# One decoder layer on one core: the last bulk rows requested behind the last regrouping, and three engines' orders rearranged

## What is computed

```
x = layernorm(x + scan_block(x))            # W_in, conv, scan over 16 states, W_out
hn = mlstm(q=x, k=ctx, v=ctx)               # decay matrix, normalizer, norm of each head, times outnorm
x = layernorm(x + hn)
logits = x @ gate_w                         # (2048, 8)
mult, sel = sparse_mixer(logits)            # top 2 experts of a token and their gates
h   = silu(x @ w1[e]) * (x @ w3[e])         # 256 -> 1024, for each expert e
out = layernorm(x + sum over 2 picks of mult * (h @ w2[e]))
```

## Time and profile before

| | us |
|---|---|
| median of the runs | 667.14 (665.72 to 668.47) |
| the profiled execution | 670.12 |
| its span, first to last instruction | 668.6 |
| PE busy | 587.2 (88%) |
| DVE busy | 456.7 (68%) |
| POOL busy | 287.2 (43%) |
| ACT busy | 249.0 (37%) |
| mean granted clock of PE | 0.926 |

### The profile page before, as it was taken

The page is one execution under the profiler, slowest core; times in us unless marked ns, Lnnn a source line. Parts: engine busy times, 40 slices in busy tenths (PEclk is TensorE's granted clock), DMA queues, the critical chain, the costliest instruction groups (busy, mean ns, idle before and its releaser), DMA issues.

```text
span 668.6 us, 13885 instructions
## 1 busy us (share of the span) xinstructions
PE 587.2 (88%) x3498; PEld 458.0 (69%) x3499; DVE 456.7 (68%) x1368; ACT 249.0 (37%) x477; POOL 287.2 (43%) x211
## 2 busy tenths in 40 slices
PE   6999989699699888537898989999999999999980
PEld 2444568588356666435687878888888888888870
DVE  2566487956566777876774766777677767677672
ACT  3555540001666653222421424224242242422262
POOL 7100020002092446646570674818576167572323
PEclk9999999899879969557899999999999999999985
DMA  8999607201300006222258475865858547544562
GB/s 269 327 335 336 196 1 203 51 1 43 147 2 1 33 9 259 81 81 95 65 132 224 98 212 146 224 157 136 223 123 232 103 94 218 146 91 94 113 195 91
DMA packets 75418, 93.42 MB, mean 140 GB/s; under 512 B 15869, under 2 KB 70270, under 8 KB 72560
## 3 DMA queue, kind: packets, MB, share of 16 engines
q1 hardware_dynamic: 63280, 78.28, 40.1%
q0 software_dynamic: 6672, 9.58, 7.3%
q10 hardware_dynamic: 5424, 5.05, 3.1%
HBM read 42.93 MB, written 31.67 MB: 112 GB/s over the span
## 4 chain that ended last, share of the span: by engine, by line
PE 63%; DVE 17%; POOL 6%; ACT 4%; DMA 3%; issue 3%; SPq 1%; another core or an unknown queue 1%; POOLq 0%; ACTq 0%; DVEq 0%
PE bank L2408 24%; PE bank L2420 13%; PE bank L1978 8%; PE bank L2137 4%; DMA xcol<-xcol 2%; POOL experts_w L861 2%; DVE region L1383 2%; DVE region L1381 2%; DVE small L1400 1%; PE bank L2028 1%; PE bank L1987 1%; PE bank L2286 1%; POOL small L780 1%; PE bank L1994 1%; PE bank L2242 1%
## 5 line engine op out<-in xcount | busy, mean ns | idle before, releaser
L2408 PE MATMUL bank<-experts_w,experts_x 128*128 (+1 forms) x864 | 215.2, 399 | 2.9 <-issue 2.9
L2408 PEld LDWEIGHTS bank<-experts_w,experts_x 128*128 128x128 f32 x864 | 157.3, 188 | 36.5 <-issue 3.7
L2420 PEld LDWEIGHTS bank<-experts_w 128*128 128x128 f32 x840 | 106.5, 194 | 6.6 <-issue 3.7
L2420 PE MATMUL bank<-experts_w 128*128 x840 | 107.7, 285 | 3.1 <-DVE region L1867 1.8
L909 POOL DMA_INDIRECT total<-region,rid x32 | 49.5, 1547 | 113.9 <-DVE region L1867 92.0
L1173 ACT ACTIVATE region<-bank 128x512 f32<-128x512 f32 x72 | 42.3, 597 | 129.2 <-PE bank L2408 115.8
L780 POOL TENSOR_TENSOR small<-small 128x4 f32<-128x4 f32 (+5 forms) x21 | 26.4, 1259 | 112.7 <-DVE small L1392 92.1
L1843 DVE TENSOR_TENSOR xcol<-region,bank 128x512 f32<-128x512 f32 x72 | 49.1, 682 | 37.1 <-ACT region L1173 37.0
L1179 ACT CAST experts_w<-bank 128x512 fp32r<-128x512 f32 x70 | 40.5, 587 | 71.7 <-DVE bank L1852 64.6
L1978 PE MATMUL bank<-xcol,region 128*128 128x512 f32 x128 | 58.1, 612 | 7.4 <-DMA xcol<-in_xT 5.8
L889 POOL TENSOR_TENSOR experts_w<-wstage,experts_w 128x2048 f32 x12 | 55.3, 4625 | 12.8 <-ACT experts_w L1197 12.8
(11 more groups left out here) (368 smaller groups left out, 933.8 us busy)
## 6 DMA issues: line engine op xcount, KB each, us to landing
wstage<-in_w_exp SPq DMA_DIRECT2D x18, 1024.0 KB, 5.2
xcol<-xcol SPq DMA_DIRECT2D x140, 128.0 KB
slots<-padrow SPq DMA_DIRECT2D x8, 2210.0 KB, 19.7
wstage<-in_w_exp SPq DMA_DIRECT2D x2, 3072.0 KB, 12.1
region<-slots ACTq DMA_DIRECT2D x34, 130.0 KB
xcol<-in_xT SPq DMA_DIRECT2D x4, 512.0 KB, 6.6
xtok<-in_x SPq DMA_DIRECT2D x1, 2048.0 KB, 13.3
region<-in_ctxT SPq DMA_DIRECT2D x1, 2048.0 KB, 7.6
```

The costliest lines, as they stand in the source:

```text
L2408: mm = pe.matmul(bank[2 * u + m][:, :], (xTh, xTl)[a][:, s, k, :], moving(off, w, m * KD * F + k * F + u * HALF, HALF), start=(k == 0 and ...
L2420: mm = pe.matmul(bank[into][:, 0:D], (high, low)[a][:, u, c, :], moving(off, w, 2 * KD * F + (4 * u + c) * D, D), start=(u == 0 and c == 0 ...
```

## The change

Six things, in the order of the program.

1. POOL's addition in `head_weights(u)` waits for `rexp_in` to reach u, for u = 1 and 2.
2. ACT's `router_exp` stands behind `weigh_keys` in the attention loop.
3. DVE's `route_place(b-2)` stands ahead of `norm2_stats(b-1)`.
4. `ENDS` is now ((0, 2), (2, 4), (6, 4), (10, 4), (14, 2)). SP has a `last_pair` of its own: it leaves out the last `load_ahead`, and requests the four groups right behind the last regrouping.
5. POOL computes the powers of the first two groups ahead of the four gathers of late rows.
6. In the last pair DVE turns block g ahead of the product of the last block, and splits block g around the first norms; ACT's norm rows are dealt out in smaller portions; PE's `last_turn(1)` stands between the two halves of `down(g)`; `end_shift(5)` stands ahead of the last late rows.

No arithmetic is added or removed. Three of the places follow as rows, each before and after. The line numbers of the changed kernel are 3 to 8 higher.

On DVE in the third turn of a sequence (c = 2), before: statistics (`BN_STATS`), then placing.

```diff
--- before.py
+++ after.py
@@ -58,7 +58,7 @@
 LOGITS_AT = {i + 1: b for i, b in TURN_AT.items()}
 RANK_AT = {i + 2: b for i, b in TURN_AT.items()}
 KEEP = 4
-ENDS = ((0, 4), (4, 4), (8, 4), (12, 2), (14, 2))
+ENDS = ((0, 2), (2, 4), (6, 4), (10, 4), (14, 2))
 LATE = 4
 LO_PARTS = 12
 LONG = 2
@@ -627,19 +627,22 @@
                 load_ahead(2 * p - 1)
                 regroup(2 * p, 0)
                 load_ahead(2 * p)
-            all_pairs(sp, pair, pair)
-
-            sp.wait_ge(w_ready, events)
-            sp.sem_inc(sp_gate, 1)
-            even = sp.value_load(tab_n[0:1, 1:2], min_val=2 * SURE - 2, max_val=NB - 2)
-            sp.wait_ge(y_sent[1], 8 * even)
-            sp.sem_inc(sp_gate, 1)
             def rows_of(t, u):
                 first, n = ENDS[u]
                 return t[first * P:(first + n) * P, :].rearrange("(i p) d -> p i d", p=P)
-            for u in range(1, len(ENDS)):
-                first, n = ENDS[u]
-                sp.dma_start(ya[:, first:first + n, :], rows_of(total, u)).then_inc(y_back[u], 16)
+
+            def last_pair(p):
+                regroup(2 * p - 1, 1)
+                load_ahead(2 * p - 1)
+                sp.wait_ge(w_ready, events)
+                sp.sem_inc(sp_gate, 1)
+                regroup(2 * p, 0)
+                sp.wait_ge(y_sent[1], 16 * p)
+                sp.sem_inc(sp_gate, 1)
+                for u in range(1, len(ENDS)):
+                    first, n = ENDS[u]
+                    sp.dma_start(ya[:, first:first + n, :], rows_of(total, u)).then_inc(y_back[u], 16)
+            all_pairs(sp, pair, last_pair)
             for u, (first, n) in enumerate(ENDS):
                 sp.wait_ge(fin_done, u + 1)
                 sp.dma_start(rows_of(out, u), ya[:, first:first + n, :]).then_inc(out_done, 16)
@@ -805,6 +808,8 @@
                 rows = hbuf[:, first % NQ:first % NQ + n].rearrange("p q h d -> p q (h d)")
                 here = xtok[:, first:first + n, 0:D]
                 link(pool.tensor_tensor(rows, rows, bc(onw[:, :], 1, [P, n, D]), ALU.mult))
+                if u:
+                    pool.wait_ge(rexp_in, u)
                 pool.tensor_tensor(here, here, rows, ALU.add).then_inc(resid_done, 1)
 
             def scatter(tiles, g):
@@ -930,11 +935,13 @@
                 pool.wait_ge(y_sent[1], 16 * p)
                 pool.sem_inc(pool_gate, 1)
                 pool.wait_ge(rid_end_done, 1)
+                for u in range(2):
+                    rsqrt(*ENDS[u][::-1])
                 for n in range(LATE):
                     pool.indirect_dma_start(out=ya[:, NT + n, :], out_offset=None, in_=total,
                                             in_offset=bass.IndirectOffsetOnAxis(ap=rid_end[:, n:n + 1], axis=0)).then_inc(gathered[n], 16)
             all_pairs(pool, pair, last_pair)
-            for first, n in ENDS:
+            for first, n in ENDS[2:]:
                 rsqrt(n, first)
             for k in range(0, LATE, 2):
                 rsqrt(2, NT + k)
@@ -1131,12 +1138,12 @@
                     decays(i + 1)
                     if c == NQ - 1:
                         states(b + 1)
-                if i in RANK_AT:
-                    router_exp(RANK_AT[i])
                 if i in TURN_AT:
                     norm2_turned(TURN_AT[i])
                 if b + 1 < B and c in (1, 2):
                     weigh_keys(b + 1, range(3 * c - 3, 3 * c))
+                if i in RANK_AT:
+                    router_exp(RANK_AT[i])
                 if b and c == NQ - 1:
                     norm2_apply(b - 1)
             norm2_turned(B - 2)
@@ -1240,16 +1247,17 @@
                 silu(last, 0)
                 act.wait_ge(grouped[0], 32 * g + 64)
                 act.sem_inc(act_gate, 1)
+                norm_rows(0, 0, 2, True)
                 plain(last, 0)
                 for u in range(2):
                     high_turned(g, u)
-                norm_rows(0, 0, 4, True)
                 silu(last, 1)
+                norm_rows(1, 2, 2, False)
                 high_end(0)
                 plain(last, 1)
-                norm_rows(1, 4, 3, False)
+                norm_rows(1, 4, 1, False)
                 high_end(1)
-                norm_rows(1, 7, 1, True)
+                norm_rows(1, 5, 1, True)
             all_pairs(act, pair, last_pair)
             for u in range(2, len(ENDS)):
                 norm_rows(u, *ENDS[u], True)
@@ -1681,9 +1689,9 @@
                     route_second(b - 2)
                     route_gates(b - 2)
                 if b and c == 2:
-                    norm2_stats(b - 1)
                     if b >= 2:
                         route_place(b - 2)
+                    norm2_stats(b - 1)
                 if b < B - 1 and c == NQ - 1:
                     if b:
                         norm2_scale(b - 1)
@@ -1931,16 +1939,16 @@
                 for u in range(2):
                     low_turned(g - 1, u, bank[4 + u], hTh, hTl)
                 end_stats(0)
-                middle(last, 1, 0)
                 for u in range(2):
                     turn(g, 0, u)
-                for u in range(2):
-                    low_turned(g, u, bank[4 + u], hTh, hTl)
                 end_shift(0)
+                middle(last, 1, 0)
                 end_stats(1)
+                low_turned(g, 0, bank[4], hTh, hTl)
+                end_shift(1)
+                low_turned(g, 1, bank[5], hTh, hTl)
                 middle(last, 1, 1)
                 low_turned(last, 0, bank[0], endTh, endTl)
-                end_shift(1)
                 end_stats(2)
                 low_turned(last, 1, bank[2], endTh, endTl)
                 end_shift(2)
@@ -1952,8 +1960,8 @@
                 end_shift(4)
                 waiting[5] = norm_stats(NT, 2, 1e-5, NT, ya)
                 late_rows(g, 2, 1)
+                end_shift(5)
                 late_rows(last, 3, 3)
-                end_shift(5)
                 waiting[6] = norm_stats(NT + 2, 2, 1e-5, NT + 2, ya)
                 end_shift(6)
             all_pairs(dve, pair, last_pair)
@@ -2481,9 +2489,9 @@
                 up(last, 1, 1, off)
                 last_turn(0)
                 off = offset_of(event_of(g))
-                for u in range(2):
-                    down(g, u, off, hTh, hTl, 1)
+                down(g, 0, off, hTh, hTl, 1)
                 last_turn(1)
+                down(g, 1, off, hTh, hTl, 1)
                 off = offset_of(event_of(last))
                 for u in range(2):
                     down(last, u, off, endTh, endTl, 3)
```

## The result

The changed kernel took 664.85 us (median of 22 runs, 662.59 to 668.21), the kernel before beside it 667.70 us (22 runs, 664.75 to 669.43). The medians are 2.9 us apart; the ratio, taken over all runs, is 0.997, 95% interval 0.9958 to 0.9982: 0.3% faster, 2.0 us, and between 1.2 and 2.8. The prediction had 662.2 us, which is 4.9 us less: the sign was right, the size about twice too large (2.5 times by the ratio, 1.7 by the medians).

What follows compares the result with a forecast made beforehand. PE bounds the expert stage; a relay between engines, with DVE held by POOL, the routing stage. 670.12 less 4.0 (routing) less 0.9 (last stage) is 665.2; the median, 3.0 lower, 662.2 us, range 660.4 to 667.2.

Steps and rivals of the forecast that it cites:

- the last stage: End of the program: earlier turn, mostly spent by a longer DVE tail, leaves 0.9 us gained.
- turn: Last stage: DVE's turn comes at 635.3 instead of 639.54, as less transfer traffic stands beside the regrouping.
- turn to last shift: Last stage: DVE's span behind the turn is 21.0 us, from 635.3 to 656.3; it was 17.90.
- last shift to first final send: Last stage: POOL's final sends also wait for bulk groups landing in out; 1.1 us gain counted as 0.9.
- The tail's work: Last stage: DVE's work behind the turn grows from 15.25 to 16.7 us by a product and larger statistics.
- the wait behind four gathers: Last stage: DVE waits 1.0 us for the power of group 2, behind four gathers on POOL.
- the routing stage: 205 to 277 us: second norm2_scale 4.6 us earlier; 4.0 us reach the stage's end, bounds 2.5 and 5.2.
- Rival (a): Routing stage: the clock falls anyway after 244, giving 2.5 us and not 4.0; 663.7 us, chance 0.18.
- rival (b): Routing stage: POOL's held additions push sends and powers, costing up to 2.1 us; 664.3 us, chance 0.12.
- Between 277 and 622 us: Relay and expert loop, forecast from 277 to 629: only start 4.0 us earlier, nothing moved; 0 us.
- (c): Relay from 277 to 350 ends on something fixed, so only the last stage gains; 666.2 us, chance 0.10.
- (d): Last stage: bulk rows share engines with the regrouping; turn at 642.5, what follows 6.6 late; 668.8 us, chance 0.10.

Runs made afterwards that it cites:

- e9: Kernel before with the three routing edits and, of the last stage, only SP's bulk-row requests right behind the last regrouping; 666.93 us, ratio 0.9949.
- e2: Changed kernel with the three routing edits undone, so the kernel before with the last-stage items only; 670.84 us, ratio 1.0011 to the kernel before.
- e5: The changed kernel, unchanged, run again in the second batch against the kernel before; 668.28 us, ratio 0.9954.
- e8: Whole change with four keep-busy matmuls also ahead of the values groups beside the logits; 671.10 us, ratio 1.0012 to the kernel before.
- e15: The whole change again, unchanged, in the fourth batch against the kernel before; 667.4 us, ratio 0.9967.
- e18: Whole change with placing ahead of norm 2's statistics only in the first sequence (b = 2); 666.49 us, ratio 0.9945 to the kernel before.
- e12: Kernel before with the three routing edits alone, second run of that program; 668.32 us, ratio 0.9985.
- e14: The kernel before, no edit, second copy of the fourth batch, against itself; 670.17 us, ratio 0.9991.
- e13: The kernel before, no edit, first copy of the fourth batch, against itself; 669.96 us, ratio 0.9998.
- e7: Whole change with POOL's four gathers ahead of all powers again; 667.25 us, ratio 0.9956 to the kernel before.
- e6: Whole change with POOL's power of the third group between the second and third gather; 667.35 us, ratio 0.9967 to the kernel before.
- e16: Kernel before with the three routing edits alone, third run of that program; 667.93 us, ratio 0.9977.
- e1: Kernel before with the three routing edits only (items 1 to 3), first run; 666.98 us, ratio 0.9939.
- e4: Kernel before with only POOL's addition waiting for rexp_in; 669.19 us, ratio 0.9961.
- e3: Kernel before with placing and keys moved, POOL's addition not waiting for rexp_in; 670.55 us, ratio 1.0007.
- e10: Kernel before with POOL's wait for rexp_in and the placing moved, keys still behind router_exp; 666.87 us, ratio 0.9958.
- e11: Kernel before with the three routing edits, but POOL's addition waiting for rexp_in only for u = 1; 668.33 us, ratio 0.9969.
- e17: Kernel before with the three routing edits, placing ahead of norm 2's statistics only in the first sequence (b = 2); 668.78 us, ratio 0.9966.

## Why the prediction was right in sign and wrong in size

**What failed first: the last stage, forecast at -0.9 us.** Eleven traces with the last stage as before (e9 among them, which differs in SP's early requests) have the turn at 10.35 to 10.99 (mean 10.64) and the end at 33.1 to 33.8 (mean 33.43). Six with the items of the change in full (after, e2, e5, e8, e15, e18) have the turn at 7.2 to 8.1 (mean 7.68) and the end at 33.3 to 34.2 (mean 33.75). By the terms of the prediction:

| | forecast | measured |
|---|---|---|
| turn | -4.2 | -3.0 |
| turn to last shift, 17.9 before | +3.1 | +2.7 |
| last shift to first final send | +0.2 | +0.6 |
| end | -0.9 | +0.3 |

The mis-sized terms are the turn and the send. "at 232 GB/s, 3.3 us from about 631, plus about 1 us to land": the regrouping took 4.58 us from its last request, at 218 GB/s, with the first rows of group 0 and SP's bulk rows beside it; the forecast turn was 2.9 us behind that request. And the final sends, "about as late as that", wait 0.56 to 0.58 us behind the last shift in every trace with these items for the bulk groups to have landed. The tail's work (16.7 forecast, 16.67 measured), the wait behind four gathers (1.0 and 1.09) and the span of 21.0 (20.58) were right. What the earlier turn gave, DVE's longer tail took, and e2 shows the sum in time: 1.0011. Why the regrouping took longer than 3.3 us and a us of landing is not shown; by e9 SP's rows alone don't delay it, and POOL's gathers came only after the turn (635.35). It is four or five small terms whose sum had the size of their errors.

**Then the routing stage, forecast at -4.0 us.** Its mechanism was right, step by step, where PE is ready at the same time: the picking at 0.19 us, no wait for bank 2, `states` to `values` in 3.43 us at clock 1.00, 0.4 us lost at line 1660 (0.3 forecast), and 4.6 and 4.1 us at the two scales (e12 against before). What failed is the last step, which carried the size of that one trace over to the median. PE's ready time differs between executions by more than the term itself (from e12 down, all rows have the three routing edits):

| | ready | scale 1 | scale 2 | from 1 to 2 |
|---|---|---|---|---|
| before | 22.83 | 31.95 | 55.40 | 23.45 |
| e14, before | 22.82 | 31.91 | 55.34 | 23.43 |
| e13, before | 24.48 | 33.47 | 56.91 | 23.44 |
| e2, routing as before | 22.06 | 31.16 | 54.60 | 23.44 |
| mean of these four | 23.05 | 32.12 | 55.56 | 23.44 |
| e12 | 22.77 | 27.39 | 51.28 | 23.89 |
| e7 | 22.76 | 27.42 | 51.28 | 23.86 |
| after | 24.41 | 29.13 | 52.93 | 23.80 |
| e5 | 19.95 | 26.82 | 50.60 | 23.78 |
| e6 | 19.97 | 26.81 | 50.58 | 23.77 |
| e15 | 19.96 | 26.81 | 50.58 | 23.77 |
| e16 | 21.21 | 26.81 | 55.31 | 28.50 |
| e1 | 27.58 | 31.93 | 55.97 | 24.04 |
| e9 | 27.54 | 31.84 | 56.69 | 24.85 |
| mean of these nine | 22.91 | 28.33 | 52.80 | 24.47 |

Before, scale 1 stands 9.0 to 9.1 us behind ready. With the edits it stands 4.3 to 4.7 behind where PE is ready at 22.7 or later, e1 and e9 included: their late scale is PE's late clock and not a gain that failed. Where PE is ready by 21.2 the scale stays at 26.8, 5.6 to 6.9 behind, because DVE's chain ends last there and PE waits 1.23 us for bank 2 in three of the four. So in the mean, with PE ready at nearly the same time (22.91 and 23.05), 3.8 us are gained at scale 1, where the prediction had 4.6. The second sequence then gives back 1.0 and not 0.6: 0.3 to 0.5 in the six traces where the clock holds, and the rest in e16, e9 and e1. That leaves 2.8 us of the 4.0, and 3.1 at POOL's first addition of the expert stage (104.3 against 107.4). With four traces against nine, whose scale 2 spreads over 6 us, this 2.8 is uncertain by about 1 us either way (an estimate from that spread); what excludes the 4.0 is the time, below.

Rival (a) had `states` at half clock in spite of the edits. That happened in none of the 15 traces with the placing moved: `states(3)` took 1.62 us in all of them, and 2.87 in all five without. A fall of the clock did take gain away, but in the second sequence (e16, 4.7 us), where no rival had it.

In time: all 36 runs of the routing edits alone have a mean of 667.92 us and all 180 of the kernel before, in the five batches, 670.05: 2.1 us (ratio 0.9958 to 0.9979 by resampling, so 1.4 to 2.8 us). That excludes 4.0. The 21 runs of the whole change in these batches have 667.05, 3.0 us (0.9939 to 0.9971). That agrees with 2.8 to 3.1 by the traces, less 0.3 for the last stage, and with the 2.0 first measured; it does not agree with 4.9. Routing edits alone and whole change can't be told apart.

**The parts of the routing gain**, at equal ready times, in scale 1: gate alone 1.8 us (e4), placing and keys without it 3.5 (e3), gate and placing 4.3 (e10 against e13), all three 4.3 to 4.6. The keys are worth nothing beside the gate. In time the shares look otherwise: the gate alone gives 2.6 us (0.9 to 4.3), as much as all three (2.1), and placing and keys without it nothing (1.0007). One trace and twelve runs of each don't settle which of the two is right. In the second sequence the gate's 2.1 us do not arrive: the sequence takes 23.8 us, and took 23.45 before. The prediction let 0.6 us go there, and 0.4 went. By e11 it comes about as 1.9 us lost to something in the edits and 1.5 regained by the second gate; e18 shows that 0.7 of the loss is the placing ahead of the statistics. That is rival (b), in part.

**Between 277 and 622 us**, forecast 0: the expert stage is the same at clock 0.99. The 2.2 us by which the profiled pair drifts further apart between 277 and 321 don't recur as a fixed term (e12 stands at 4.1 us at scale 2 and at 4.1 at POOL's first addition).

**Rivals (c) and (d).** (c), nothing but the last stage gains, is excluded: it is the other way round. (d), the bulk rows delay the turn, is excluded by e9 (turn at 10.44, and at 10.35 to 10.99 without them) and by the turn at 7.2 to 8.1 in the whole change. The sum of (d) has a slip that decides nothing: 631 + 11.3 is 642.3, and the us of landing that the forecast adds is left out of it.

**What stays open.** Whether the edits change how often the clock falls: of 15 traces with the placing moved, four have a long fall in the second sequence, clock 0.50 to 0.53 from 252 to 270 (e3, e8, e16, e17), of five without it none (before, e2, e4, e13, e14); e9 and e4, one of each kind, have a shorter one, 0.72. That is too few to settle it, and if the edits do bring the fall on, it is part of why 4.0 became 2.1. Open too is what holds `before` back where PE is ready ahead of 22: no trace of it shows that. No version here beats the whole change by more than the intervals; e18 (0.9945), whose trace shows the wait gone, would be the one to keep, but its time does not show it better.

## What to carry to other kernels

Where a stage hangs on a clock that differs between executions, price an edit in several of them: two or three traces of the kernel before, with no edit, show in which of them the wait that goes away was the last one to end, and the gain is the mean over these, not the value of the one trace at hand. Set two traces side by side only where the stage was entered at the same time: e1 beside before looks like no gain, and yet its scale stands 4.35 us behind PE's ready time, where before needed 9.12. An engine that is held by another's memory access is freed by moving that access behind the chain, but what reads the result of the moved instruction is the next bound; move only where something waits. And a sum of small terms of both signs in a last stage (-4.2, +3.1, +0.2) is known no better than the errors of its terms: forecast it as nothing, with its spread.
